# Counting edges in rings of six chunks, chunk totals in registers, five-row corrections widened to 96 rows, and the output bias added ahead

## The chip, the cores and the metric

The kernel runs on one core of a Trainium2 chip. The metric is the device time of one execution in microseconds (us), lower is better. The core has five engines that run side by side and meet at semaphores: TensorE (PE in the profile; its weight loads are PEld), VectorE (DVE), ScalarE (ACT), GpSimd (POOL) and SyncE (SP), which issues the DMAs.

## What is computed

A graph of N = 1250 nodes with 512 features and E = 21250 edges, sorted by destination. Four layers of conditioned layer norm, sparse four-head attention over the edges and a two-layer MLP come first; two graph convolutions follow. Cut to what matters here:

```python
x, src, dst, node_vec1 = _rec_inputs()         # (1250, 512), edges sorted by dst
h = jnp.maximum(_layernorm(x, axis=-1), 0.0)
x = x + _L0_gnn_ref(h, edge_index, ...)        # 4 blocks: attention over edges, MLP
h = jnp.maximum(_layernorm(x, axis=-1), 0.0)
x = x + _L1_gnn_ref(h, edge_index, W1, b1, W2, b2)

def _gcn_conv(x, src, dst, W, b, n):           # used twice, relu between
    h = x @ W
    deg = segment_sum(ones, dst)
    norm = rsqrt(deg)[src] * rsqrt(deg)[dst]
    return segment_sum(h[src] * norm, dst) + b
```

Edges are random pairs, so the kernel never gathers by edge. It first makes a dense 1250 x 1250 matrix that says how often each edge occurs, and both the attention and the graph convolutions are then dense products with it.

## The kernel before, in words

**Counting (span 12 to 175 us).** The nodes are ten tiles of 125, the edges 170 chunks of 125. A tile of destinations needs the chunks that hold them, found at run time: `tab` holds for each tile its first chunk and its number of turns, and for each tile from the third on the turns of earlier tiles of the same parity. For each chunk VectorE makes two one-hot matrices in bf16, `oh_dst` (125 edges x 125 nodes, L1105) and `oh_src` (125 edges x 1250 nodes, L1107), and TensorE multiplies them into a 125 x 1250 count in PSUM with three matmuls of 512, 512 and 226 columns (L1622). One turn of the loop (`one_hots` on VectorE, `count_tile` on TensorE) does `TRIO` = 3 chunks, so the chunks of a tile are rounded up to a multiple of three; surplus chunks count nothing. Even tiles use one ring of three slots, odd tiles another, so VectorE may be at most three chunks ahead within a tile, and it may begin the next tile with three chunks of the other ring. It waits on `oh_used0` or `oh_used1`, which TensorE raises after a chunk; TensorE waits on `onehot0` or `onehot1`.

Between two tiles TensorE closes the sum (L1627), turns the counts of the tile before into blocks (L1639), opens the next sum (L1610) and does one small matmul of the conditioning network (L1659, up to the eighth tile); ScalarE copies counts and blocks out, and SP writes the blocks to `counts_scratch` in DRAM. VectorE reads numbers of `tab` into registers (`value_load`, L1096 to L1098: three of them from the third tile on) and has small work of its own: the sines' arguments after the first tile, splits of the weights after the fifth to seventh, the first layer norm around the last two.

**The four layers (175 to 1640 us)** are not touched.

**The graph convolutions (1640 to 1885 us).** Float32 values go through TensorE as pairs of fp32r halves. The count matrix with self loops (`whole`) is one fp32r half; what is cut off is nonzero only in rows with large counts, at most `WIDE` = 5 rows, and that rest is one more small product. `gather_rows(j, p)` (L1903) is the first convolution's gather: for each of four feature groups j and three column pieces p, 20 matmuls of 125 rows. `add_rest(j, p)` (L1910) adds the rest with one matmul of 5 rows from `hs5[0]` and `rest5`. `last_rows(t)` (L1975) and `last_rest(t)` (L1980) do the same for the second convolution, once per node tile, with `hs5[1]`. Between them lies the product with the second weight (`product`, L1680), for which `rows_out` on ScalarE and `rows_low` on VectorE (L1381) make the two halves. GpSimd adds the self loops (L606) and fetches the five rows by index (L679). At the end VectorE scales each tile, adds the output bias `bvb` into `ztmp` (L1570), adds that to the running features `z` (L1573), and SP writes the tile out. TensorE goes on with tile t once `g_fin` says that bank t - 2 was read.

Each engine runs its instructions in the order written; nothing reorders them.

Of the kernel before, what the change touches and what calls it, by code (L numbers as in the profile page):

```python
# [14 lines left out]
ALU = mybir.AluOpType  # L15
# [9 lines left out]
N = 1250  # L25
# [5 lines left out]
C = 16  # L31
# [7 lines left out]
TRIO = 3  # L39
ECP = EC + TRIO  # L40
# [14 lines left out]
WIDE = 5  # L55
WIDE_AT = 4095.5


def build(nc, x, src, dst, node_vec1, f_w1, f_b1, f_w2, f_b2, s1_w, s1_b, b1_w, b1_b, wq, bq, wk, bk, wv, bv,
# [5 lines left out]
    with ExitStack() as ctx:  # L65
# [134 lines left out]
        rest5 = place("rest5", [WIDE, N], F32R, r_qg)  # L200
        hs5 = [place("hs5a", [WIDE, D], F32R, r_qc), place("hs5b", [WIDE, D], F32R, r_qg + 5024)]
# [12 lines left out]
        h1T = early("h1T", [C, N])  # L214
        oh_src = early("oh_src", [T, 2 * TRIO, N], BF16)
        oh_dst = early("oh_dst", [T, 2 * TRIO, T + 1], BF16)
        iota16 = early("iota16", [T, N], F16)
        iota_i = early("iota_i", [T, N], I32)
        zeros16 = early("zeros16", [T, D], BF16)
        edge_i = early("edge_i", [128, 4, T], I32)  # L220
        edge_f = early("edge_f", [128, 4, T])
        edgeT = early("edgeT", [T, 2, ECP])
        nb = early("nb", [2 * NFREQ, N])
# [45 lines left out]
        for name in ("x_ld edge_ld small_ld brow_ld ident consts edge_f edge_t edgeT brow_t cols emb_u emb_r emb_f emb emb_h "  # L269
# [7 lines left out]
                     "g_agT g_w2h g_w2 g_row g_tri g_wide g_gath g_h5 g_h5e g_b5 g_ft g_fin g_fz g_out z0 settled").split():  # L277
# [188 lines left out]
        def _(pool):  # L466
# [3 lines left out]
            for ring in range(2):  # L470
                pool.sem_inc(s[f"oh_used{ring}"], TRIO)
# [204 lines left out]
            for t in range(6, NT):  # L676
                self_loop(t)
            pool.wait_ge(s["g_wide"], 5)
# [349 lines left out]
        def _(dve):  # L1028
# [52 lines left out]
            tab_step(v.tensor_scalar(tab[:, 0:NT], R[2], float(ECP - TRIO), None, ALU.min))  # L1081
            tab_step(v.tensor_scalar(R[1], R[4], 1.0 / TRIO, 1.0 / TRIO, ALU.mult, ALU.add))
# [9 lines left out]

            def one_hots(t):

                ring = t % 2
                first = dve.value_load(tab[0:1, t:t + 1], min_val=0, max_val=ECP - TRIO)  # L1096
                trios = dve.value_load(tab[0:1, NT + t:NT + t + 1], min_val=1, max_val=EC // TRIO + 1)
                before = 0 if t < 2 else dve.value_load(tab[0:1, 2 * NT + t:2 * NT + t + 1], min_val=0, max_val=(EC // TRIO + 1) * NT)  # L1098
                with dve.Fori(0, trios) as i:
                    used = dve.snap((before + i) * TRIO)  # L1100
                    chunk0 = dve.snap((first + i * TRIO).with_bounds(min_val=0, max_val=ECP - TRIO))
                    for b in range(TRIO):
                        slot = ring * TRIO + b
# [432 lines left out]
            dve.wait_ge(s["g_b5"], 1)  # L1536
# [27 lines left out]
            for t in range(NT):  # L1564
                rows_low(NT + t, t % 2, t)
# [452 lines left out]
```

## Time and profile before

| | us |
|---|---|
| median of three runs | 1888.9 (1887.29 to 1889.1) |
| the profiled execution | 1887.38 |
| its span | 1885.5 |
| TensorE busy | 1823.2 (97%) |
| VectorE busy | 1382.1 (73%) |
| ScalarE busy | 826.0 (44%) |
| GpSimd busy | 450.9 (24%) |
| mean granted TensorE clock | 0.995 |

The profile is of one execution. TensorE is busy nearly throughout, so a microsecond is gained where TensorE waits, or where a group of its instructions takes longer than its columns need. The page cuts the span into 40 slices of 47 us; the first four show TensorE at 6, 9, 9 and 9 tenths, and the rest 9 or more but for the last. A busy time is not a peak, since matmuls overlap, so starts are a better measure of pace than durations.

### The profile page before, as it was taken

The page shows a single profiled execution, that of the slowest core. Times are in us where ns is not written, and L with a number is a line of the kernel's source. Part 1 is how long each engine was busy: PE and PEld are TensorE (multiplying, and loading weights), DVE is VectorE, ACT ScalarE, POOL GpSimd, SP SyncE. Part 2 cuts the span into 40 slices and gives each one's busy share as a digit, 9 for nine tenths or more (in the row PEclk, how much of TensorE's full clock was granted, in tenths as well). Part 3 has the DMA queues.
Part 4 walks back from the last instruction along what each step waited for, and adds up shares of the span by engine and source line. Part 5 has one row for each costly group of instructions (what it writes and reads, how often), then busy time and mean ns, then how long its engine had stood idle before and what let it go on. Part 6 is the DMA issues. An engine that isn't in the chain of part 4 may idle for free. (4 is left out here: it accounts for less than half of the span.)

```text
span 1885.5 us, 33968 instructions
## 1 busy us (share of the span) xinstructions
PE 1823.2 (97%) x11796; PEld 1570.6 (83%) x11796; DVE 1382.1 (73%) x2835; ACT 826.0 (44%) x1613; POOL 450.9 (24%) x544
## 2 busy tenths in 40 slices
PE   6998999999999999999999999999999999999998
PEld 3555988999889989998899899988998999877776
DVE  7887669888885498888854988888549888875323
ACT  1552455455442264554422555544225555446220
POOL 1000234111351341113513411125134111261000
PEclk9999999999999999999999999999999999999999
DMA  4112563111301121103011211030112110522001
GB/s 142 40 40 54 156 171 116 38 37 28 125 1 56 39 61 38 37 27 127 1 56 38 60 38 37 27 127 1 49 46 61 38 37 27 161 52 54 1 1 55
DMA packets 50752, 108.40 MB, mean 57 GB/s; under 512 B 18170, under 2 KB 18222, under 8 KB 50640
## 3 DMA queue, kind: packets, MB, share of 16 engines
q1 hardware_dynamic: 50608, 106.87, 19.4%
q8 instruction: 72, 1.18, 0.3%
q14 instruction: 40, 0.33, 0.1%
q0 software_dynamic: 32, 0.03, 0.0%
HBM read 83.62 MB, written 23.25 MB: 57 GB/s over the span
## 5 line engine op out<-in xcount | busy, mean ns | idle before, releaser
L871 ACT ACTIVATE PT<-ps 125x500 fp32r<-125x500 f32 (+1 forms) x480 | 214.2, 520 | 315.6 <-PE ps L1780 315.6
L1680 PE MATMUL ps<-PT,V 125*128 125x250 f32 x2400 | 313.3, 284 | 1.6 <-DVE PT L1279 1.6
L1680 PE MATMUL ps<-kT,qg 128*125 128x512 f32 (+1 forms) x1440 | 302.2, 355 | 6.1 <-DVE nmx L1263 5.2
L1680 PEld LDWEIGHTS ps<-kT,qg 128*125 128x125 f32 x1440 | 245.8, 187 | 55.4 <-issue 6.8
L1680 PEld LDWEIGHTS ps<-PT,V 125*128 125x128 f32 x2400 | 289.6, 190 | 2.9 <-DVE PT L1279 2.9
L1279 DVE TENSOR_TENSOR PT<-ps,PT 125x500 fp32r<-125x500 f32 (+1 forms) x480 | 253.2, 583 | 2.2 <-ACT PT L871 1.8
L1263 DVE CUSTOM_DVE_ANT_0 SB<-ps,bt 125x1250 f32<-125x1250 f32 x140 | 203.9, 1457 | 46.7 <-PE ps L1680 44.6
L1780 PE MATMUL ps<-ident,pbuf 125*125 125x125 f32 x1600 | 202.2, 274 | 10.3 <-DVE PT L1279 4.0
L1780 PEld LDWEIGHTS ps<-ident,pbuf 125*125 125x125 f32 x1600 | 187.3, 189 | 14.0 <-issue 9.3
L865 ACT ACTIVATE pbuf<-SB,nmx 125x1250 f32<-125x1250 f32 x140 | 188.1, 1344 | 11.0 <-DVE nmx L1263 9.7
L1272 DVE TENSOR_SCALAR pbuf<-pbuf,rden 125x1250 f32<-125x1250 f32 x160 | 149.9, 937 | 5.6
L542 POOL CAST qg<-qc 128x250 fp32r<-128x250 f32 x80 | 36.2, 453 | 443.4 <-PE ps L1680 408.3
L1680 PEld LDWEIGHTS ps<-yTb,wa 128*128 128x128 f32 x1152 | 136.7, 189 | 3.1 <-issue 1.3
L1680 PE MATMUL ps<-yTb,wa 128*128 128x250 f32 x1152 | 137.2, 279 | 1.1 <-DVE yTb L1228 1.1
L1622 PE MATMUL ps<-oh_src,oh_dst 125*125 125x512 bf16 x558 | 122.6, 374 | 9.4 <-DVE oh_src L1107 9.4
L1680 PE MATMUL ps<-wmS,hT 128*125 128x512 f32 x480 | 124.3, 403 | 3.4 <-POOL hT L613 3.1
L1622 PEld LDWEIGHTS ps<-oh_src,oh_dst 125*125 125x125 bf16 x558 | 67.3, 145 | 67.0 <-DVE oh_src L1107 45.1
L1680 PEld LDWEIGHTS ps<-yT,wmS 128*128 128x128 f32 x960 | 114.1, 189 | 4.2 <-issue 2.4
L1680 PE MATMUL ps<-yT,wmS 128*128 128x250 f32 x960 | 114.6, 278 | 2.0 <-DVE yT L1228 2.0
L1680 PEld LDWEIGHTS ps<-wmS,hT 128*125 128x125 f32 x480 | 84.6, 186 | 32.0 <-POOL hT L613 11.2
L1680 PE MATMUL ps<-WOS,outTg 128*125 128x512 f32 x320 | 102.3, 401 | 0.3
L1107 DVE TENSOR_SCALAR oh_src<-iota,edgeT 125x1250 bf16<-125x1250 f16 x186 | 101.9, 548 | 0.0
(243 smaller groups left out, 2811.0 us busy)
## 6 DMA issues: line engine op xcount, KB each, us to landing
bt<-edge_bias_scratch SPq DMA_DIRECT2D x40, 546.9 KB
q_scratch<-qc SPq DMA_DIRECT2D x16, 500.0 KB, 2.6
qc<-q_scratch SPq DMA_DIRECT2D x16, 500.0 KB, 4.7
counts_scratch<-cblk SPq DMA_DIRECT2D x10, 546.9 KB
c_rows<-counts_scratch SPq DMA_DIRECT2D x10, 546.9 KB
edge_bias_scratch<-b_rows SPq DMA_DIRECT2D x10, 546.9 KB
counts<-counts_scratch SPq DMA_DIRECT2D x10, 546.9 KB
wm<-in_L_gnn_wo_dram SPq DMA_DIRECT2D x4, 1024.0 KB, 8.6
```

The costliest lines, as they stand in the source:

```text
L542: g.tensor_copy(qg[:, 0, h, :], qc[:, h, :]).then_inc(s["qgh"], 1)
L865: sc.activation(P[:, u, :], SB[:, :] if own else P[:, u, :], ACT.Exp, bias=nmx[:, u:u + 1], scale=-1.0, accum_out=den[:, u:u + 1]).then_in ...
L871: sc.activation(PT[:, h % 2, 0, a:b, u * T:(u + 1) * T], ps_T[0:T, i, 0:(b - a) * T].rearrange("p (t n) -> p t n", n=T), ACT.Copy).then_in ...
L1107: v.tensor_scalar(oh_src[:, slot, :], iota16[:, :], edgeT[:, 0, bass.ds(chunk0 + b, 1)], None, ALU.is_equal).then_inc(s[f"onehot{ring}"], 1)
L1263: v.tensor_tensor_reduce(out=SB[:, :] if own else P[:, u, :], in0=banks, in1=bt[:, u, :], scale=-1.0, scalar=FLOOR, op0=ALU.add, op1=ALU.m ...
L1272: v.tensor_scalar(P[:, u, :], P[:, u, :], rden[:, u:u + 1], None, ALU.mult).then_inc(s["P"], 1)
L1279: v.tensor_tensor(o[:, 1], ps_T[0:T, i, 0:(b - a) * T].rearrange("p (t n) -> p t n", n=T), o[:, 0].bitcast(F32), ALU.subtract).then_inc(s[ ...
L1622: e = mm(psf[0:T, o + a:o + b], oh_dst[:, slot, 0:T], oh_src[:, slot, a:b], start=False, stop=False, skip_group_check=True)
L1680: e = mm(out_, lhs(a), rhs(b), start=start and i == 0, stop=stop and i == 2)
L1780: e = turn(ps_T[0:T, p, (m - a) * T:(m - a + 1) * T], P[:, u, m * T:(m + 1) * T], ident[0:T, 0:T])
```

## The change

Three things change.

1. `TRIO` becomes `SIX` = 6: a turn does six chunks, a ring has six slots, the chunks of a tile are rounded up to a multiple of six. VectorE no longer loads the earlier turns from `tab`; it adds the turn counts that it has in registers. TensorE still loads them. To make room `h1T`, `iota_i`, `edge_i` and `nb` move to memory that is used only later.
2. `rest5` and both `hs5` get `DEEP` = 96 rows, cleared to zero by GpSimd; VectorE writes five rows of them as before. The matmuls of L1910 and L1980 then have 96 rows. VectorE waits for the clearing (`g_z5`) ahead of its first copy into `wide_y`, which shares memory with `rest5`.
3. `z` gets the output bias tile by tile during the product with the second weight; at the end one instruction does `z = ps * dis + z` in place of two, and TensorE waits for `g_fz` in place of `g_fin`.

The diff, without the moved placements and the renamings:

```diff
-            tab_step(v.tensor_scalar(R[1], R[4], 1.0 / TRIO, 1.0 / TRIO, ALU.mult, ALU.add))
+            tab_step(v.tensor_scalar(R[1], R[4], 1.0 / SIX, 0.5 - 0.5 / SIX, ALU.mult, ALU.add))
...
+            turns, done_by = [], [0, 0]
+
             def one_hots(t):
 
                 ring = t % 2
-                first = dve.value_load(tab[0:1, t:t + 1], min_val=0, max_val=ECP - TRIO)
-                trios = dve.value_load(tab[0:1, NT + t:NT + t + 1], min_val=1, max_val=EC // TRIO + 1)
-                before = 0 if t < 2 else dve.value_load(tab[0:1, 2 * NT + t:2 * NT + t + 1], min_val=0, max_val=(EC // TRIO + 1) * NT)
-                with dve.Fori(0, trios) as i:
-                    used = dve.snap((before + i) * TRIO)
...
+                first = dve.value_load(tab[0:1, t:t + 1], min_val=0, max_val=ECP - SIX)
+                sixes = dve.value_load(tab[0:1, NT + t:NT + t + 1], min_val=1, max_val=EC // SIX + 1)
+                before = done_by[t] if t < 2 else dve.snap((done_by[t] + turns[t - 2]).with_bounds(min_val=0, max_val=(EC // SIX + 1) * NT))
+                turns.append(sixes)
+                done_by.append(before)
+                with dve.Fori(0, sixes) as i:
+                    used = dve.snap((before + i) * SIX)
...
             for t in range(6, NT):
                 self_loop(t)
+            g.memset(hs5[0][:, :].bitcast(F32), 0.0).then_inc(s["g_z5"], 1)
+            pool.wait_ge(s["g_hs_mm"], NT)
+            g.memset(rest5[:, :].bitcast(F32), 0.0).then_inc(s["g_z5"], 1)
+            g.memset(hs5[1][:, :].bitcast(F32), 0.0).then_inc(s["g_z5"], 1)
             pool.wait_ge(s["g_wide"], 5)
...
             dve.wait_ge(s["g_b5"], 1)
+            dve.wait_ge(s["g_z5"], 3)
             for p, (a, b) in enumerate(PIECES):
                 e = v.tensor_copy(wide_y[:, a * T:b * T], ps[0:WIDE, 3 + p, 0:(b - a) * T])
...
             for t in range(NT):
                 rows_low(NT + t, t % 2, t)
+                v.tensor_tensor(z[:, t, :], z[:, t, :], bvb[:, :], ALU.add).then_inc(s["g_fin"], 1)
             dve.wait_ge(s["g_h5"], 2)
-            v.tensor_copy(hs5[1][:, :], ps[0:WIDE, 2, :]).then_inc(s["g_h5e"], 1)
+            v.tensor_copy(hs5[1][0:WIDE, :], ps[0:WIDE, 2, :]).then_inc(s["g_h5e"], 1)
             for t in range(NT):
                 dve.wait_ge(s["g_ft"], t + 1)
-                v.scalar_tensor_tensor(out=ztmp[:, t % 2, :], in0=ps[0:T, t % 2, :], scalar=dis[:, t:t + 1], in1=bvb[:, :],
-                                       op0=ALU.mult, op1=ALU.add).then_inc(s["g_fin"], 1)
                 dve.wait_ge(s["g_fin"], t + 1)
-                v.tensor_tensor(z[:, t, :], z[:, t, :], ztmp[:, t % 2, :], ALU.add).then_inc(s["g_fz"], 1)
+                v.scalar_tensor_tensor(out=z[:, t, :], in0=ps[0:T, t % 2, :], scalar=dis[:, t:t + 1], in1=z[:, t, :],
+                                       op0=ALU.mult, op1=ALU.add).then_inc(s["g_fz"], 1)
...
-                    pe.wait_ge(s["g_fin"], t - 1)
+                    pe.wait_ge(s["g_fz"], t - 1)
```

How instructions stand on VectorE where the third tile's one-hots begin, before the change (TENSOR_LOAD and the ISA rows behind it are one `value_load`; the last rows are the first chunk):

```order
L1096 TENSOR_LOAD tab
L1096 ISA x2
L1097 TENSOR_LOAD tab
L1097 ISA x2
L1098 TENSOR_LOAD tab
L1098 ISA x2
L1099 UNCONDITIONAL_BRANCH
L1099 ISA
L1105 ISA
L1105 TENSOR_SCALAR oh_dst<-iota_148,edgeT 125x125
```

And with the change:

```order
L1103 TENSOR_LOAD tab
L1103 ISA x2
L1104 TENSOR_LOAD tab
L1104 ISA x2
L1108 UNCONDITIONAL_BRANCH
L1108 ISA
L1114 ISA
L1114 TENSOR_SCALAR oh_dst<-iota_148,edgeT 125x125
```

One of the three loads is gone. The rows of the loop behind it repeat a chunk six times in place of three.

GpSimd's last rows, before:

```order
L606 TENSOR_TENSOR counts_107<-counts_107,ident 125x125
L606 TENSOR_TENSOR counts_108<-counts_108,ident 125x125
L606 TENSOR_TENSOR counts_109<-counts_109,ident 125x125
L606 TENSOR_TENSOR counts_110<-counts_110,ident 125x125
L679 DMA wide_x<-counts_scratch,idx 5x1250
```

And with the change:

```order
L607 TENSOR_TENSOR counts_110<-counts_110,ident 125x125
L679 MEMSET hs5a 96x512
L681 MEMSET rest_134 96x1250
L682 MEMSET hs5b 96x512
L684 DMA wide_x<-counts_scratch,idx 5x1250
```

Three clears stand between the last self loop and the fetch of the five rows.

VectorE's end of the program, before (`agg_low`'s last row, the ten of `rows_low`, the five rows for the rest, then each tile's two steps):

```order
L1554 TENSOR_TENSOR aggL<-agg_123,aggH 128x226
L1381 SCALAR_TENSOR_TENSOR hsL<-ps,dis,hsH 125x512 x10
L1567 CAST hs5b<-ps 5x512
L1570 SCALAR_TENSOR_TENSOR ztmp<-ps,dis,bvb 125x512
L1573 TENSOR_TENSOR z<-z,ztmp 125x512
```

And with the change:

```order
L1390 SCALAR_TENSOR_TENSOR hsL<-ps,dis,hsH 125x512
L1576 TENSOR_TENSOR z<-z,bvb 125x512
L1578 CAST hs5b<-ps 5x512
L1582 SCALAR_TENSOR_TENSOR z<-ps,dis,z 125x512 x10
L66 UNCONDITIONAL_BRANCH
```

The ten additions to `z` moved from behind the last matmuls to between the ten steps of `rows_low`.

## Rows read from the trace of the kernel before

**Rows 1.** The page: busy time, share of the span and instructions.

```profile
PE 1823.2 (97%) x11796; PEld 1570.6 (83%) x11796; DVE 1382.1 (73%) x2835; ACT 826.0 (44%) x1613; POOL 450.9 (24%) x544
```

**Rows 2.** Counting: us, busy PE PEld DVE ACT POOL, clock, DMA share, GB/s.

```profile
12.00:175.00 163.00, 147.57 (x705) 82.45 (x706) 136.80 (x409) 59.61 (x111) 1.45 (x2) 0.96 0.23 63
```

**Rows 3.** Timeline of DVE, third tile: start, duration, engine, line, [idle before <- releaser].

```profile
47.05 0.26 DVE L1105 TENSOR_SCALAR oh_dst<-iota,edgeT 125x125 bf16<-125x125 f16 x1 [1.69 <-issue]
...
51.00 0.26 DVE L1105 TENSOR_SCALAR oh_dst<-iota,edgeT 125x125 bf16<-125x125 f16 x1 [2.00 <-PE ps L1622]
51.17 0.54 DVE L1107 TENSOR_SCALAR oh_src<-iota,edgeT 125x1250 bf16<-125x1250 f16 x1
...
59.81 0.54 DVE L1107 TENSOR_SCALAR oh_src<-iota,edgeT 125x1250 bf16<-125x1250 f16 x1
```

**Rows 4.** Timeline of PE and PEld, end of the third tile, start of the fourth.

```profile
60.40 0.41 PEld L1622 LDWEIGHTS ps<-oh_src,oh_dst 125*125 125x125 bf16 x3 [0.21 <-DVE oh_src L1107]
...
64.91 1.47 PEld L1622 LDWEIGHTS ps<-oh_src,oh_dst 125*125 125x125 bf16 x9 [0.85 <-DVE oh_src L1107]
64.91 11.16 PE L1622 MATMUL ps<-oh_src,oh_dst 125*125 125x512 bf16 x54
```

**Rows 5.** Waits by line, VectorE: us in total, times, longest.

```profile
DVE oh_dst L1105 <- PE ps L1622: 11.6, 19, 2.0
```

**Rows 6.** Timelines of DVE and PE where the clock was low.

```profile
19.93 0.26 DVE L1105 TENSOR_SCALAR oh_dst<-iota,edgeT 125x125 bf16<-125x125 f16 x1 [0.32 <-PE ps L1622]
20.98 0.26 DVE L1105 TENSOR_SCALAR oh_dst<-iota,edgeT 125x125 bf16<-125x125 f16 x1 [0.34 <-PE ps L1622]
...
127.64 13.74 PE L1622 MATMUL ps<-oh_src,oh_dst 125*125 125x512 bf16 x54 [2.07 <-DVE oh_src L1107]
...
146.67 14.37 PE L1622 MATMUL ps<-oh_src,oh_dst 125*125 125x512 bf16 x63 [2.44 <-DVE oh_src L1107]
```

**Rows 7.** Sequencer instructions of lines 1098 (DVE) and 1616 (PE): duration ns min/median/max.

```profile
L1098 DVEq TENSOR_LOAD <-tab x8: 298/298/311, 46.0 to 162.2; - x8
L1098 DVEq FUSED_REGOPS  x8: 183/183/183, 46.4 to 162.6; - x8
L1098 DVEq SEQ_ASSERT  x8: 23/23/23, 46.6 to 163.2; - x8
L1616 PEldq COMPARE_BRANCH  x62: 76/207/241, 17.7 to 175.0; - x62
```

**Rows 8.** The chain that ended last, first convolution's gather: start, us, what.

```profile
1739.99 4.63 PE ps L1903 x20
...
1776.69 0.42 PE ps L1910
1777.11 4.83 PE ps L1903 x20
1781.94 0.42 PE ps L1910
```

**Rows 9.** Timeline of PE: matmuls of 96 rows among matmuls of 128 rows.

```profile
207.99 1.11 PE L1691 MATMUL ps<-lnS,condc 96*125 96x512 f32 x4
208.94 0.97 PE L1680 MATMUL ps<-yT,wa 128*128 128x250 f32 x7
```

**Rows 10.** GpSimd's last self loop and a 96-row clear; VectorE's first copy into wide_y.

```profile
1714.18 0.46 POOL L606 TENSOR_TENSOR counts<-counts,ident 125x125 f32<-125x125 f32 x1 [1.38 <-DMA counts<-counts_scratch]
...
L505 POOL MEMSET condS<- 96x1250 f32 x1 | 1.1, 1141 | 0.1
...
1756.28 1.57 DVE L1538 COPY wide_y<-ps 5x500 f32<-5x500 f32 x3 [4.42 <-PE ps L1936]
```

**Rows 11.** Timeline of DVE: rows_low's last step, and the end of the program.

```profile
1827.13 0.75 DVE L1381 SCALAR_TENSOR_TENSOR hsL<-ps,dis,hsH 125x512 fp32r<-125x512 f32 x1 [2.04 <-ACT hsH L925]
...
1881.35 0.75 DVE L1570 SCALAR_TENSOR_TENSOR ztmp<-ps,dis,bvb 125x512 f32<-125x512 f32 x1 [3.78 <-PE ps L1980]
1882.13 0.69 DVE L1573 TENSOR_TENSOR z<-z,ztmp 125x512 f32<-125x512 f32 x1
```

More of the change, by code:

```diff
@@ L199, in build @@
         wide_y = place("wide_y", [WIDE, N], F32, r_qg)
-        rest5 = place("rest5", [WIDE, N], F32R, r_qg)
-        hs5 = [place("hs5a", [WIDE, D], F32R, r_qc), place("hs5b", [WIDE, D], F32R, r_qg + 5024)]
+        rest5 = place("rest5", [DEEP, N], F32R, r_qg)
+        hs5 = [place("hs5a", [DEEP, D], F32R, r_qc), place("hs5b", [DEEP, D], F32R, r_qg + 5024)]
         in_pb = packer(r_pb + 4 * 4 * D, r_pb + 4 * 2 * N)
@@ L276, in build @@
                      "g_cnt g_c6 g_c7 g_c8 g_c9 g_x zx g_xd g_nb g_eye g_H g_dg g_diag g_bc g_disb g_hs_mm g_hh g_hs g_ag g_agd g_agr g_agh "
-                     "g_agT g_w2h g_w2 g_row g_tri g_wide g_gath g_h5 g_h5e g_b5 g_ft g_fin g_fz g_out z0 settled").split():
+                     "g_agT g_w2h g_w2 g_row g_tri g_wide g_gath g_h5 g_h5e g_b5 g_ft g_z5 g_fin g_fz g_out z0 settled").split():
             s[name] = sem(name)
@@ L470, in _ @@
             for ring in range(2):
[L471 removed]
+                pool.sem_inc(s[f"oh_used{ring}"], SIX)
             g.memset(ident[:, :], 0.0).then_inc(s["ident"], 1)
@@ L1091, in _ @@
             dve.wait_ge(s["prefix"], 3)
+            turns, done_by = [], [0, 0]
             def one_hots(t):
                 ring = t % 2
[L1096 to L1103 removed]
+                first = dve.value_load(tab[0:1, t:t + 1], min_val=0, max_val=ECP - SIX)
[5 more added lines that the diff above has]
+                    used = dve.snap((before + i) * SIX)
+                    chunk0 = dve.snap((first + i * SIX).with_bounds(min_val=0, max_val=ECP - SIX))
+                    for b in range(SIX):
+                        slot = ring * SIX + b
                         dve.wait_ge(s[f"oh_used{ring}"], used + (b + 1))
@@ L1611, in open_counts, with count_tile @@
                        skip_group_check=True)
-            def count_tile(t, trios, before):
+            def count_tile(t, sixes, before):
                 ring, o = t % 2, ACC[t % 2]
-                with pe.Fori(0, trios) as i:
-                    done = pe.snap((before + i) * TRIO)
-                    for q in range(TRIO):
-                        slot = ring * TRIO + q
+                with pe.Fori(0, sixes) as i:
+                    done = pe.snap((before + i) * SIX)
+                    for q in range(SIX):
+                        slot = ring * SIX + q
                         pe.wait_ge(s[f"onehot{ring}"], done + (q + 1))
@@ L1663, in _ @@
                 open_counts(t)
-                ahead = trios_ahead(t)
+                ahead = sixes_ahead(t)
                 if t >= 2:
```

29 lines of the change are left out of this document (15 added, 14 removed).

## The prediction, written before the changed kernel ran

> **What bounds the kernel now.** I read the page first: TensorE is busy for 97% of the span, VectorE for 73% [rows 1], so over the whole program TensorE is the bound. The change touches the counting and the last 150 us, so I went on by stretch. In the counting [rows 2] TensorE is busy 147.6 of 163 us and VectorE 136.8, so neither is plainly the bound, and the timeline has to tell. It shows VectorE going from chunk to chunk in 0.617 us ((59.81 - 51.17) / 14) [rows 3], with TensorE behind it, idle 0.21 us before each chunk's first weight load [rows 4]: within a tile VectorE sets the pace. Between tiles it is otherwise. VectorE makes three chunks of the next tile, then waits 2.00 us for a slot [rows 3], since TensorE begins the tile 4.51 us after its last chunk began (64.91 - 60.40) [rows 4]. So a full tile takes neither engine's own time but the sum of pieces of both: the third tile starts on VectorE at 47.05 and the fourth 1.7 us after 60.35 (59.81 + 0.54), 15.0 us apart, of which 18 chunks are 11.1 [rows 3]. The waits for slots are 11.6 us in 19 times [rows 5]. From 1740 us on the chain is TensorE alone [rows 8], with one step of VectorE at its end [rows 11].
>
> **Deeper rings.** How many chunks there are: 186 before, eight tiles of 18 and two of 21 (x54 and x63 are three matmuls per chunk) [rows 4, 6]. A tile of 18 needed 16 to 18, one of 21 needed 19 to 21; in sixes these become 18 and 24. That adds 6 chunks of 0.617: +3.7 us.
>
> Waits removed: the 11.6 us are idle time alone. A normal chunk starts 0.09 us before the one ahead ends (0.617 against 0.17 + 0.54) [rows 3], which a wait loses too, and some waits are too short to be listed; start against start, over all 186 pairs, I get 14.2 us. Of these 7.3 stand at the starts of tiles 3 to 7 (2.1 at the third, 51.00 - 47.05 - 3 x 0.617 [rows 3], then 2.0, 1.4, 1.6 and 0.2), and 6.9 in stretches in which TensorE ran at 1.2 GHz. There a chunk takes it 1.05 us (20.98 - 19.93) [rows 6] against 0.617 on VectorE, and three slots are soon full. Each such stretch lasted four to seven chunks, so TensorE falls back by at most 7 x 0.43 = 3.0 us, which three more slots (1.9 us) and the slack of the first three nearly cover: I count all 6.9 us as removed.
>
> At the starts of tiles not all goes. At full clock TensorE needs 0.50 us per chunk by its weight loads (9 in 1.47) [rows 4], and 0.57 if I count the columns at the float32 gather's pace (4.63 / 20 per 512) [rows 8]; I take 0.53, between the two. A tile then costs TensorE at least 4.51 + 17 x 0.53 = 13.5 us, and VectorE 18 x 0.617 + about 1.2 for its register loads = 12.3. So in tiles 3 to 6 TensorE becomes the bound and VectorE waits again at its seventh chunk: with six chunks made (3.7 us) and a slot free about 1.0 us after TensorE has begun the tile, I get 0.85, 1.2, 0.6 and 0.2 us, in all 2.8. From the seventh tile on VectorE's own insertions and the extra chunks keep it behind, and it does not wait. Removed, then: 14.2 - 2.8 = 11.4 us.
>
> What could eat into this is TensorE's own loop: a backward branch is 0.21 us on its sequencer [rows 7], which is hidden now because TensorE waits for VectorE anyway. With some bookkeeping it is up to 0.3 us for each of three turns in four tiles, 3.5 us in all; I take nothing, since the branches are issued while queued matmuls still run, and keep 3.5 for the range. On the other side 0.50 us per chunk would give at most 17 x 0.03 x 4 = 2 us more.
>
> **Turn counts in registers.** One value_load less is 0.298 + 0.183 + 0.023 us [rows 7] and the gaps between; three of them and the branch make the 1.69 us idle [rows 3], so one is 0.5 to 0.6: I take 0.58. It counts at eight tile starts, but twice it lies under a split of 2.29 us that is still running, so 6 x 0.58 = 3.5 us less. The addition in its place is one register operation. If the queue in front of VectorE hid the load, it would be worth nothing; the 1.69 us of idle says that it does not.
>
> Counting together: -11.4 - 3.5 + 3.7 = -11.2 us. What follows (GpSimd's wait for the last blocks in DRAM, the first layer's loads) hangs on the last tile and moves with it. The moved placements only take memory whose users come later in program order; I cost them at 0, and their semaphores are the old ones.
>
> **96 rows.** A rest matmul of 5 rows begins at 1776.69 and the next at 1781.94, 5.25 us for 20 gather matmuls and one rest; at the pace of the first run (4.63 for 20, 0.2315 each) 21 would take 4.86 [rows 8]. So each place where 5-row matmuls stand among 125-row ones costs 0.39 us, for one or for three in a row, by going in and coming out. There are 17 such places: 8 in the first gather (two groups of three, six alone) and 9 in the last (a pair, eight alone), and the last has no way out. 96 rows do not show this: four of 96 rows among 128-row matmuls take 0.95 us, 0.2375 each [rows 9]. So 16 x 0.385 + 0.19 = 6.3 us less, all of it on TensorE's chain. The bounds are 0 (if the 96-row row does not carry over) and 6.6.
>
> The Trainium skill speaks against this step. By its page TensorE: Matmul & The Clock Gate, section "Why this matters for your kernels", a lone matmul of 32 rows takes the time of one of 128, so the row count alone should buy nothing. By that rule this term would be 0 and the whole 6.3 us smaller in gain; the starts in rows 8 disagree for 5 rows between 125-row neighbours, and I go by them.
>
> GpSimd's clears: its last self loop ends at 1714.6, a 96 x 1250 clear takes 1.14 us, one of 512 columns about 0.5 [rows 10]. The first is free at once; the other two wait for the last `nodes` product, which ends at 1739.99 where the gather begins [rows 8], so they are over by 1741.7. VectorE needs them at 1756.28 [rows 10], 14.6 us later. Behind the clears only the fetch of five rows is queued on GpSimd, and it waits for the same engine's index until 1752. Cost 0; were the cover gone, TensorE's second feature group would wait too, since it needs the banks that VectorE copies out.
>
> **Bias ahead.** Ten additions of 0.69 us [rows 11] go between the steps of rows_low, which take 0.75 us and stand 2.8 us apart with 2.04 idle [rows 11]. They fit: 1.44 of 2.8. The last ends before 1829, and VectorE's next work (five rows of hs5) came at 1833.4. Cost 0; without that cover, 6.9 us. At the end one step of 0.69 us and its gap go: 1882.13 - 1881.35 = -0.8 us. That TensorE waits for g_fz in place of g_fin is the same instruction's end.
>
> **The sum.** -11.2 - 6.3 - 0.8 = -18.3 us on an execution of 1887.4 us (span 1885.5): 1869.1. The median of the runs shown is 1.5 us above the profiled execution, so I forecast 1870.6 us.
>
> **Rivals.** (a) *TensorE's turns show.* With more chunks ready TensorE is the bound and its branches cost the 3.5 us above: 1874.1. For it: TensorE never ran more than a few chunks unhindered here, so its loop has not been seen at full pace. Against it: half as many branches.
> (b) *96 rows gain nothing*, because the cost is in changing the operands' source and not in five rows: 1876.9. Against it: rows 9.
> (c) *Slower: the low clock stays.* In the counting TensorE fell to 1.2 GHz after it had stood idle for 2.07 and for 2.44 us [rows 6]. If the new rhythm kept it low, a tile would take 18 x (1.05 - 0.617) = 7.8 us more. It decides from the third such tile on (18.3 / 7.8 = 2.3); with five it is 1909 us. Against it: the waits of TensorE become shorter, and in tiles 3 to 6 there are none.
> (d) *The rings bring nothing*: something else holds a tile at 15 us, for instance ScalarE's copies between tiles; then only the load, the 96 rows and the bias gain, and 3.7 are lost: 1870.6 + 11.4 = 1882.0. Against it: VectorE's waits name TensorE's matmuls of the same ring.
>
> **Chances and range.** The forecast 0.74, (a) 0.11, (b) 0.07, (c) 0.03, (d) 0.03, and 0.02 for no difference. The forecast's own range is 1867.5 to 1873.5: 2 us for the pace per chunk and 1 for the load. To hold 8 of 10 I go up to (b) and down by one stretch of low clock that no longer comes: 1866 to 1877. A change of this kernel can be told from none by 0.2%, 3.8 us. Faster 0.95 (all but (c) and the last), same 0.02, slower 0.03.
>
> **What would show it.** In the changed profile: 192 pairs of one-hots, VectorE's waits on the counting matmuls down from 11.6 us to some 3 and only at a tile's seventh chunk; 1.1 us idle by issue at tile starts; the counting over 11 us earlier; from one rest matmul to the next 4.86 us; the last steps on VectorE one of 0.75 us. The prediction is wrong if the seventh chunk waits longer than 1.5 us, if the stretch from the first gather matmul to the end is not 7 us shorter, or if TensorE runs the counting at half clock.

## The result, and the profile after

The changed kernel takes 1871.03 us (median of 4 runs, 1869.86 to 1872.21) against 1889.0 us for the kernel before on the same chip (4 runs, 1887.29 to 1889.28): ratio 0.9908, 95% interval 0.9895 to 0.992. That is 18 us less, and the forecast was 1870.6. The profiled execution took 1871.84 us with a span of 1870.1 (before: 1887.38 and 1885.5), so between the two profiles the difference is only 15.5 us. Step by step, as markers in the two traces (us from the span's start):

| | before | after | shift |
|---|---|---|---|
| last pair of one-hots begins on VectorE | 174.14 | 162.19 | -11.95 |
| TensorE's conditioning chunk behind the count blocks' landing (L1701) begins | 189.46 | 178.95 | -10.51 |
| first convolution's gather begins | 1739.83 | 1729.60 | -10.23 |
| W2's product begins | 1798.25 | 1786.68 | -11.57 |
| last gather begins | 1826.21 | 1814.56 | -11.65 |
| last step of VectorE ends | 1882.83 | 1867.39 | -15.44 |

First the page of the changed kernel, its busy times and counts, beside [rows 1]:

```profile
PE 1810.0 (97%) x11814; PEld 1575.5 (84%) x11814; DVE 1382.6 (74%) x2847; ACT 826.5 (44%) x1613; POOL 453.8 (24%) x547
```

TensorE runs 18 matmuls more (six extra chunks) and still is 13 us less busy, VectorE has 12 operations more. (In the page of the kernel before, the fourth of the 40 slices shows TensorE at 8 tenths, not 9; with the change the first four are 6, 9, 8 and 8.) The counting by stretch, as in [rows 2], the same columns:

```profile
12.00:175.00 163.00, 148.40 (x791) 94.65 (x792) 144.67 (x436) 65.76 (x125) 1.82 (x2) 0.98 0.28 71
```

In the same 163 us 86 more matmuls fit in, since the first layer has begun by then; VectorE's busy time rises from 136.8 to 144.7. The waits of VectorE, by line, over the counting (us in total, times, longest), which answer [rows 5]:

```profile
DVE oh_dst L1114 <- issue: 6.8, 7, 1.9
DVE oh_dst L1114 <- PE ps L1632: 4.7, 3, 1.9
```

Nineteen waits for slots are now three, and they are where the prediction put them, at the seventh chunk of tiles 3, 4 and 5. But look at how long they are, and at what is missing ahead of the tiles. VectorE's timeline with the change, the waits of tiles 3 to 5, to be set beside [rows 3] (start, duration, line, in brackets the idle time before):

```profile
48.05 0.26 DVE L1114 TENSOR_SCALAR oh_dst<-iota,edgeT 125x125 bf16<-125x125 f16 x1 [1.94 <-PE ps L1632]
...
55.82 0.26 DVE L1114 TENSOR_SCALAR oh_dst<-iota,edgeT 125x125 bf16<-125x125 f16 x1 [0.26 <-issue]
...
61.30 0.26 DVE L1114 TENSOR_SCALAR oh_dst<-iota,edgeT 125x125 bf16<-125x125 f16 x1 [1.69 <-PE ps L1632]
...
69.22 0.26 DVE L1114 TENSOR_SCALAR oh_dst<-iota,edgeT 125x125 bf16<-125x125 f16 x1 [0.35 <-issue]
...
74.07 0.26 DVE L1114 TENSOR_SCALAR oh_dst<-iota,edgeT 125x125 bf16<-125x125 f16 x1 [1.05 <-PE ps L1632]
```

The third tile has no idle time at its start at all (it begins at 42.33, six chunks of 0.617 before the wait), the fourth and fifth 0.26 and 0.35 us, where there were 1.7 us before. TensorE's weight loads of the third tile and its matmuls, answering [rows 4]:

```profile
47.05 9.47 PEld L1632 LDWEIGHTS ps<-oh_src,oh_dst 125*125 125x125 bf16 x54 [0.85 <-issue]
```

```profile
47.05 9.81 PE L1632 MATMUL ps<-oh_src,oh_dst 125*125 125x512 bf16 x54
...
60.29 5.99 PE L1632 MATMUL ps<-oh_src,oh_dst 125*125 125x512 bf16 x32
```

Eighteen chunks in one unbroken group of 54: 9.47 / 18 = 0.53 us each, through three turns of the loop. From the third tile to the fourth TensorE takes 60.29 - 47.05 = 13.2 us instead of 15.

The first gather, its chain in order of time (start, us, what), beside [rows 8]:

```profile
1736.46 6.30 PE ps L1913 x20
...
1762.64 4.65 PE ps L1913 x20
1767.29 0.24 PE ps L1920
1767.52 4.64 PE ps L1913 x20
1772.16 0.24 PE ps L1920
```

From one rest matmul to the next it is 1772.16 - 1767.29 = 4.87 us, against 5.25 before; the rest matmul itself counts 0.24 us instead of 0.42. The first row shown is a trap: 20 gather matmuls in 6.30 us, because the granted clock stood at its lower level (1.2 GHz) for 3.4 us from 1737.7 on. GpSimd's clears, by start, duration and line, answering [rows 10], read 1705.60 0.52 (L679), 1729.82 1.14 (L681) and 1730.90 0.53 (L682): the last two began as the gather began, and VectorE did not wait for them. And VectorE at the end, answering [rows 11]:

```profile
1815.48 0.75 DVE L1390 SCALAR_TENSOR_TENSOR hsL<-ps,dis,hsH 125x512 fp32r<-125x512 f32 x1 [1.44 <-ACT hsH L930]
1816.15 0.68 DVE L1576 TENSOR_TENSOR z<-z,bvb 125x512 f32<-125x512 f32 x1
...
1861.79 0.75 DVE L1582 SCALAR_TENSOR_TENSOR z<-ps,dis,z 125x512 f32<-125x512 f32 x1 [4.13 <-PE ps L1990]
1866.64 0.75 DVE L1582 SCALAR_TENSOR_TENSOR z<-ps,dis,z 125x512 f32<-125x512 f32 x1 [4.10 <-PE ps L1990]
```

The bias additions sit in what was idle time, and the steps of the last gather are 4.85 us apart.

### The profile page after: what moved, and what is told of

Read it like the earlier page. It is cut to its first block and busy times, and to the rows that moved or that the text cites. A ratio compares the mean times of both kernels' runs of the same rounds, so it can differ in the third digit from the quotient of the medians.

```text
span 1870.1 us, 33910 instructions
## 1 busy us (share of the span) xinstructions
PE 1810.0 (97%) x11814; PEld 1575.5 (84%) x11814; DVE 1382.6 (74%) x2847; ACT 826.5 (44%) x1613; POOL 453.8 (24%) x547
## 5 line engine op out<-in xcount | busy, mean ns | idle before, releaser
L1690 PEld LDWEIGHTS ps<-yTb,wa 128*128 128x128 f32 x1152 | 136.8, 189 | 3.1 <-issue 1.3
L1632 PE MATMUL ps<-oh_src,oh_dst 125*125 125x512 bf16 (+1 forms) x576 | 115.4, 358 | 6.9 <-DVE oh_src L1116 6.9
L1632 PEld LDWEIGHTS ps<-oh_src,oh_dst 125*125 125x125 bf16 x576 | 71.1, 142 | 53.3 <-DVE oh_src L1116 26.0
```

Source lines behind the costliest of these rows:

```text
L1632: e = mm(psf[0:T, o + a:o + b], oh_dst[:, slot, 0:T], oh_src[:, slot, a:b], start=False, stop=False, skip_group_check=True)
L1690: e = mm(out_, lhs(a), rhs(b), start=start and i == 0, stop=stop and i == 2)
```

## The experiments

Twelve kernels ran, in three groups of four, each group on a chip of its own; the kernel before ran with each group (medians 1886.73, 1886.48 and 1888.13 us). A figure in brackets is the 95% interval of a ratio to it.

### Each part alone

**The rings alone** (with the turn counts in registers and the moved placements; the rest as before; lines of the edit against the changed kernel):

```diff
-        rest5 = place("rest5", [DEEP, N], F32R, r_qg)
+        rest5 = place("rest5", [WIDE, N], F32R, r_qg)
...
-                v.tensor_tensor(z[:, t, :], z[:, t, :], bvb[:, :], ALU.add).then_inc(s["g_fin"], 1)
```

> The kernel before with the rings of six and the turn counts in registers alone; 5-row rests and the two last steps as before. My theory: the trace of the changed kernel has its last pair of one-hots 12.0 us earlier than before, of which 1.4 us were lost again behind it, when TensorE waited 1.79 in place of 0.43 us for GpSimd and the last blocks in DRAM. If that loss is the ring's doing (blocks arrive closer together), this kernel gains 10.5 us: 1878.5. If it is chance of one execution, it gains up to 12: 1877. By rival (d) of the prediction it gains nothing or loses: 1885 or more. The wait for the last blocks in its profile tells the first two apart: 1.8 us again, or 0.4.

Measured: 1876.42 us, ratio 0.9947 [0.9934, 0.996], so 10.3 us less. Its last pair begins at 162.16, as in the full change, with the same two waiting rows (6.8 and 4.7 us). The question about the last blocks is answered too: here they land 6.55 us after their copy, and TensorE does not wait at that chunk, so the 1.79 us of the first profile are not the ring's doing. The gather has the row of 6.30 us.

**96 rows alone** (kernel before, with the diff's hunks on `rest5`, `hs5` and the three clears):

```diff
-            v.tensor_copy(hs5[0][:, :], ps[0:WIDE, 6, :]).then_inc(s["g_h5e"], 1)
+            v.tensor_copy(hs5[0][0:WIDE, :], ps[0:WIDE, 6, :]).then_inc(s["g_h5e"], 1)
```

> The kernel before with the 96-row rests alone. My theory: 17 places lose 0.385 us each, 6.1 to 6.3 us less, 1882.8; from one rest matmul to the next 4.87 us. By rival (b), the row count alone buys nothing: 1889. A second question is the stretch of low clock that the changed kernel had in the gather, 1737.7 to 1741.1 us, which cost it 1.6 us: if the 96 rows bring it, it is here too, at the same place in the program; if it hangs on what happened before, it is not, and the gain is the full 6.2.

Measured: 1880.92 us, 0.9967 [0.9954, 0.998], 5.8 us less. Its chain in the first gather:

```profile
1771.65 4.65 PE ps L1909 x20
1776.30 0.24 PE ps L1916
1776.53 4.64 PE ps L1909 x20
1781.17 0.24 PE ps L1916
```

The 4.87 us from rest to rest come with this edit and nothing else. The second question of the expectation, the low clock in the gather, is answered by a row further ahead in the same chain:

```profile
1745.47 6.30 PE ps L1909 x20
```

The granted clock is at its lower level for 3.4 us from 1746.8 on, 8.2 us behind the gather's start and at the same place in the program as in the changed kernel. So in this profile too the first gather has 1.6 us of the gain taken back.

**The bias alone:**

```diff
+                v.tensor_tensor(z[:, t, :], z[:, t, :], bvb[:, :], ALU.add).then_inc(s["g_fin"], 1)
...
-                v.tensor_tensor(z[:, t, :], z[:, t, :], ztmp[:, t % 2, :], ALU.add).then_inc(s["g_fz"], 1)
+                v.scalar_tensor_tensor(out=z[:, t, :], in0=ps[0:T, t % 2, :], scalar=dis[:, t:t + 1], in1=z[:, t, :],
+                                       op0=ALU.mult, op1=ALU.add).then_inc(s["g_fz"], 1)
```

> The kernel before with the output bias added ahead alone. My theory: 0.7 to 0.8 us less, 1888.2, below what can be measured in the median, but plain in the profile as one step of 0.75 us at the end in place of 0.75 and 0.69. A rival: the ten additions get in the way of the steps of rows_low or of the last matmuls, and it is slower by more than 1 us.

Measured: 1885.39 us, 0.9995 [0.9987, 1.0004]: 1.3 us less, with an interval that holds both no change and the 0.8 us expected. The three parts add up to 10.3 + 5.8 + 1.3 = 17.4 us, the whole change gives 18.0: no interaction between them shows above the noise.

**The full change with the register load put back:**

```diff
-                before = done_by[t] if t < 2 else dve.snap((done_by[t] + turns[t - 2]).with_bounds(min_val=0, max_val=(EC // SIX + 1) * NT))
+                before = 0 if t < 2 else dve.value_load(tab[0:1, 2 * NT + t:2 * NT + t + 1], min_val=0, max_val=(EC // SIX + 1) * NT)
```

> The changed kernel with the third register load put back (rings of six and all else stay). The prediction's term: 6 exposed loads of 0.58 us, 3.5 us slower than the changed kernel, 1874.5. The rival from the changed trace: in tiles 3 to 6 TensorE is the bound, so there the load is hidden by the six chunks that are ready or by the wait at the seventh; only the last three tiles are set by VectorE, and it costs 3 x 0.6 = 1.8 us, 1872.9. The wait at the seventh chunk tells: if it shrinks by the load's 0.6 us in tiles 3 to 5, the rival is right.

Measured: 1870.37 us, 0.9917 [0.9904, 0.9929]: 16.4 us less than before where the full change has 18.0. The medians differ by less than the intervals; the traces are sharper. The last pair begins at 164.14 instead of 162.19, 1.95 us later. The start of tile 4 and its seventh chunk in this kernel, then the starts of tiles 8 to 10:

```profile
56.44 0.26 DVE L1114 TENSOR_SCALAR oh_dst<-iota,edgeT 125x125 bf16<-125x125 f16 x1 [0.86 <-issue]
61.33 0.26 DVE L1114 TENSOR_SCALAR oh_dst<-iota,edgeT 125x125 bf16<-125x125 f16 x1 [1.08 <-PE ps L1632]
...
118.77 0.26 DVE L1114 TENSOR_SCALAR oh_dst<-iota,edgeT 125x125 bf16<-125x125 f16 x1 [2.15 <-issue]
135.29 0.26 DVE L1114 TENSOR_SCALAR oh_dst<-iota,edgeT 125x125 bf16<-125x125 f16 x1 [2.12 <-issue]
153.65 0.26 DVE L1114 TENSOR_SCALAR oh_dst<-iota,edgeT 125x125 bf16<-125x125 f16 x1 [1.72 <-issue]
```

The starts of tiles 8 to 10 in the changed kernel:

```profile
118.22 0.26 DVE L1114 TENSOR_SCALAR oh_dst<-iota,edgeT 125x125 bf16<-125x125 f16 x1 [1.64 <-issue]
...
134.23 0.26 DVE L1114 TENSOR_SCALAR oh_dst<-iota,edgeT 125x125 bf16<-125x125 f16 x1 [1.61 <-issue]
...
151.70 0.26 DVE L1114 TENSOR_SCALAR oh_dst<-iota,edgeT 125x125 bf16<-125x125 f16 x1 [0.84 <-issue]
```

Tile 4 is the lesson. With the third load 0.86 + 1.08 = 1.94 us are idle, without it 0.26 + 1.69 = 1.95 (rows above): the load was paid out of the wait behind it, and the seventh chunk begins at 61.33 or 61.30. Only in the last three tiles, where VectorE is the late engine, does it show: 2.15, 2.12 and 1.72 us against 1.64, 1.61 and 0.84, in all 1.9 us. This is what the expectation's rival said, and not the prediction's term.

### The depth of the ring and the rounding

Both edit one number of the full change:

```diff
-SIX = 6
+SIX = 3
```

> The changed kernel with three chunks per turn and three slots per ring again, turn counts still in registers, 96-row rests and early bias kept: it takes the depth away and the rounding with it. My theory after the first four runs: the depth is nearly all of the counting's gain. With three slots the starts of tiles 3 to 7 are held by the slot wait whatever the loads cost, so the missing load shows in tiles 8 to 10 only. Expected: last one-hot pair at 170 to 172.5 us (the kernel before: 172 to 174.1 in three profiles; the changed kernel 162.1), 186 pairs, waits for slots 11 to 12 us again, the whole 8.5 us slower than the changed kernel, 1878.5. By the prediction's term (six loads exposed, 3.5 us) it would be only 6.5 slower.

Measured for three: 1877.4 us, 0.9952 [0.9938, 0.9965]. VectorE's waits, and its operations:

```profile
L1116 DVE TENSOR_SCALAR oh_src<-iota,edgeT 125x1250 bf16<-125x1250 f16 x186 | 101.5, 546 | 0.0
L1114 DVE TENSOR_SCALAR oh_dst<-iota,edgeT 125x125 bf16<-125x125 f16 x186 | 47.2, 254 | 24.4 <-PE ps L1632 14.2 <-issue 9.5
```

Slots are waited for 22 times again, 14.2 us, and the last pair begins at 174.60, later than the 170 to 172.5 expected. At the third tile the two waits are now

```profile
47.56 0.26 DVE L1114 TENSOR_SCALAR oh_dst<-iota,edgeT 125x125 bf16<-125x125 f16 x1 [1.08 <-issue]
...
52.12 0.26 DVE L1114 TENSOR_SCALAR oh_dst<-iota,edgeT 125x125 bf16<-125x125 f16 x1 [2.61 <-PE ps L1632]
```

against 1.69 and 2.00 before [rows 3]: the load is gone from the first and comes back in the second. The same trade stands at tiles 4 and 5. At tiles 8 to 10 the idle time falls from 2.15, 2.11 and 1.70 to 1.66, 1.62 and 0.83 us, 1.85 us that no slot wait takes back. That the last pair is late all the same goes in part with the clock, which was at its lower level five times for 3.4 us in this counting and four times in that of the kernel before; the rest is not separated. By medians the edit leaves 9.1 us of gain, of which 96 rows and bias are 7.1, so the load is at most 2; the depth and its rounding are then worth the other 8.9 of the 18.0 us (expected 8.5).

```diff
-SIX = 6
+SIX = 5
```

> The changed kernel with five chunks per turn and five slots. Tiles of 16 to 18 chunks become 20, those of 19 to 21 become 20 or 25: 200 to 210 pairs. It prices the rounding. If a surplus chunk costs VectorE's 0.617 us throughout, 8 more pairs (200) put the last pair 4.9 us later than in the changed kernel, at 167.1, and 18 more (210) at 173.2; if surplus chunks are free where TensorE is the bound they would cost less, but there TensorE's own 0.53 per chunk holds, 4.3 and 9.5 us. A loss well above 0.62 per extra pair would mean that a fifth slot is not enough and depth still counts.

Measured for five (2 runs): 1877.37 us, 0.9952 [0.9934, 0.9971]. The same two rows:

```profile
L1116 DVE TENSOR_SCALAR oh_src<-iota,edgeT 125x1250 bf16<-125x1250 f16 x200 | 108.6, 543 | 0.0
L1114 DVE TENSOR_SCALAR oh_dst<-iota,edgeT 125x125 bf16<-125x125 f16 x200 | 51.6, 258 | 13.9 <-PE ps L1632 7.1 <-issue 6.5
```

Five slots leave more waiting for slots than six (7.1 against 4.7 us; idle by issue is 6.5 against 6.8), and a tile of 16 to 18 chunks rounded up to fives takes 20, so 200 pairs are made: 8 x 0.617 = 4.9 us more. The last pair begins at 170.08, 7.9 us later than with six, or 0.99 us per extra pair. That is well above 0.62, so by the expectation's own test depth still counts: of the 3.0 us beyond the rounding 2.4 are slot waits, now at the sixth chunk (2.55, 2.37 and 1.30 us in tiles 3 to 5). Six is good here because it is deeper and because 18 is a multiple of it.

### How many rows a lone matmul must have

```diff
-DEEP = 96
+DEEP = 32
```

> The changed kernel with the rests cleared to 32 rows in place of 96. If what costs is how few rows the rest has, 32 rows should be nearer to 96 than to 5. If what costs is a way of using the array that goes with up to 32 rows, the rest of 32 rows costs the same as that of 5: 0.39 us at each of 17 places, 5.25 us from one rest to the next, 6.1 us slower than the changed kernel.

Measured (2 runs): 1876.72 us, 0.9949 [0.9931, 0.9967]. Its chain in the first gather:

```profile
1760.12 4.83 PE ps L1913 x20
1764.95 0.42 PE ps L1920
1765.37 4.83 PE ps L1913 x20
1770.20 0.42 PE ps L1920
```

> The changed kernel with the rests cleared to 64 rows. By the theory that a smaller part of the array is used and the change between parts costs, 64 rows (half) cost as much as 32, 5.25 us from rest to rest; by the theory that the cost falls with the rows, it is between 4.87 and 5.25.

With `DEEP = 64` (2 runs): 1874.8 us, 0.9939 [0.9921, 0.9957], and

```profile
1760.53 4.84 PE ps L1913 x20
1765.37 0.42 PE ps L1920
1765.79 4.83 PE ps L1913 x20
1770.62 0.42 PE ps L1920
```

From rest to rest it is 5.25 us with 32 rows and with 64, the same as with 5. From the first gather matmul to VectorE's last step it is 143.9 us with 32 rows, in an execution with the row of 6.30 us, and 142.4 with 64, in one without it; with 96 rows it is 137.8 with that row (changed kernel) and 136.2 without (the kernel with the load put back): 6.1 us between them in both pairs, as expected. The medians, of two runs each, are 5.7 and 3.8 us above that of the changed kernel. So what costs 0.39 us is no matter of how few rows there are: 64 rows, 59 of them zero, gain nothing, 96 gain all. The Trainium skill, page TensorEngine Tiling (Array Packing), section "Tiling Modes", says that changing the tiling mode drains TensorE. The three depths agree with that, if 96 rows run in the mode of 125 and 64 do not; the page gives no duration, and here it is 0.39 us for going in and coming out.

### The changed kernel again, and two ways on

> The changed kernel once more, as the measure for the three kernels beside it and to see what an execution of it can vary. Theory: its counting ends at the same place each time (last one-hot pair at 162.1 us), while the landing of the last count blocks (9.0 us in the first profile, 6.6 to 7.5 in other kernels) and the number of 3.4 us stretches at the low clock differ from one execution to the next; so the median is again 1869 to 1873 us and the profiled execution may lie 1 to 3 us to either side of it. Rival: the 9.0 us landing and the low-clock stretch at the head of the gather belong to this kernel; then this profile shows both again, at 8.5 us or more and within 10 us of the gather's start.

Measured: 1870.25 us (1869.95 to 1871.03), 0.9908 [0.9892, 0.9925]. The last pair begins at 162.15. From the last block's copy to GpSimd's operation behind its landing it is 7.39 us here, 9.02 in the first profile; TensorE's wait at that place is 0.17 instead of 1.79. So the theory holds for the landing. For the low clock the rival holds: the stretch is there again, from 1736.1 on, 8.1 us behind the gather's start as in the first profile, and so is the one 58 us ahead of it (1678.1 here, 1679.7 there). Two executions of two are no proof that it belongs to the kernel, but it is no single accident.

**Loads ahead of their tiles.** If a load is free where VectorE's sequencer is ahead of its engine, the three exposed starts can be cured by their place in the code:

```diff
+            def load_turns(t):
...
+                if t not in ready:
+                    load_turns(t)
+                first, sixes, before = ready[t]
...
                 if t == 6:
+                    load_turns(7)
                     node_rstd()
                 if t == 7:
                     cond_low()
+                    load_turns(8)
+                    load_turns(9)
```

> VectorE's register loads of the last three tiles are issued earlier: those of tile 8 ahead of the square-root steps of the node statistics, those of tiles 9 and 10 (counted from one) right behind the conditioning row's low part. Theory: a load costs nothing where VectorE's sequencer is ahead of its engine, and 1.64, 1.61 and 0.84 us are idle at the starts of these three tiles only because the sequencer has caught up there. With the loads under long operations the idle time falls to a loop start of some 0.3 us each: last pair at 159 to 160 us, median 2.5 to 3.5 us under the changed kernel beside it. Rival: these tiles are held by TensorE all the same (it is at most a ring behind), so what VectorE gains is waited away at the seventh chunk: last pair at 161.5 or later and under 1 us gained.

Measured: 1866.3 us (1866.15 to 1866.53), 0.9887 [0.987, 0.9903]. The starts of tiles 8 and 9 in this kernel:

```profile
116.89 0.26 DVE L1123 TENSOR_SCALAR oh_dst<-iota,edgeT 125x125 bf16<-125x125 f16 x1 [0.38 <-issue]
131.89 0.26 DVE L1123 TENSOR_SCALAR oh_dst<-iota,edgeT 125x125 bf16<-125x125 f16 x1 [0.35 <-issue]
```

0.38 and 0.35 us where there were 1.64 and 1.61, and no gap at tile 10. The waits for slots stay at 4.7 us and the last pair begins at 158.91, 3.24 us earlier: the theory, and the rival falls. Of the 3.95 us between the medians these 3.24 are explained; the rest is within what the low clock moves (the stretch at the gather's head is absent here, which is 1.6 us in the profile).

**GpSimd's wait for the count blocks one chunk later:**

```diff
+                    if l == 0 and n == 0:
+                        for i in range(2):
+                            pool.wait_ge(s[f"cnt_out{i}"], NT * 16)
                     v_split(l, n)
...
-            for i in range(2):
-                pool.wait_ge(s[f"cnt_out{i}"], NT * 16)
```

> GpSimd's wait for the landing of the count blocks stands one conditioning chunk later, so that its first operation of layer 0 no longer stands behind it. Theory: in the changed kernel's profile TensorE waits 1.79 us for that operation because the landing took 9.0 us; where the landing takes about 6.7 us the wait is 0.4 to 0.9 us. Moved, the wait is gone whatever the landing takes: median 0.4 to 1.8 us under the changed kernel beside it, 0.9 likeliest. Rival: the next thing TensorE needs is late by the same amount (the low part of the first normalised block, written by VectorE), and nothing is gained: within 0.4 us.

Measured: 1868.54 us (1868.14 to 1869.11), 0.99 [0.9883, 0.9916], 1.7 us under the changed kernel beside it. TensorE at this place, in this kernel and then in the changed kernel's first profile:

```profile
171.28 5.87 PE L1691 MATMUL ps<-yTb,wa 128*128 128x250 f32 x48 [1.12 <-DVE yTb L1238]
176.99 1.08 PE L1702 MATMUL ps<-lnS,condc 96*125 96x512 f32 x4
```

```profile
171.29 5.87 PE L1690 MATMUL ps<-yTb,wa 128*128 128x250 f32 x48 [1.12 <-DVE yTb L1237]
178.95 1.19 PE L1701 MATMUL ps<-lnS,condc 96*125 96x512 f32 x4 [1.79 <-POOL condc L527]
```

The wait is gone. Against the profile of the changed kernel beside it (177.31) that is only 0.3 us, so most of the 1.7 us are not this wait: 1.6 us of the profiles' difference are again the low clock at the gather's head, absent here. Worth of the wait: 0.3 to 1.9 us, by how long the landing takes.

> The loads ahead and GpSimd's wait later, in one kernel. Theory: the two places lie one behind the other in time and add up: 3 + 0.9 = 3.9 us under the changed kernel beside it, so 1866 to 1868.5 us, the fastest of all here. Rival: with the counting over earlier the weights' and conditioning's preparation on GpSimd and ScalarE is late instead, and of the 3.9 us less than 2 are left.

Measured: 1866.75 us (1865.45 to 1869.59), 0.9894 [0.9878, 0.9911]. That is 3.5 us under the changed kernel beside it and inside the expected 1866 to 1868.5, but not the fastest of all: it cannot be told from the loads alone. In the profiles the two do add (last pair 158.85; conditioning chunk at 173.58 against 174.41; end at 1860.97 against 1861.79), so 0.8 us are there and drown in these four runs. In this execution the gather ran at the higher level of the clock (2.4 GHz):

```profile
1731.60 4.74 PE ps L1926 x20
```

That row answers the 6.30 above. The two kernels with the loads ahead are the fastest of all here, faster than both the kernel before and the changed one.

## Why the prediction came true, and which terms were off

*What bounds.* Right. A tile took pieces of both engines, and with six slots tiles 3 to 5 are TensorE's: 12.8 to 13.2 us from start to start, forecast 13.5.

*Counting: forecast -11.2, measured -12.0.* Two errors nearly cancel.

- The rings were forecast at -11.4 + 3.7 = -7.7 us. Measured without the load's part (the kernel with the load put back, last pair 164.14 against 174.14) they give -10.0. The step that failed is "in all 2.8" for the waits that stay, and more than that what stands at the tiles' starts: I left all idle time by issue as it was. With three loads per tile and six slots VectorE waits 3.5 us for slots (0.7 more than forecast), but idle by issue falls from 13.0 to 9.8 us (3.2 less).
- The load was forecast at -3.5 and is worth -2.0. The sentence "the 1.69 us of idle says that it does not" (hide) was the mistake: it read the shallow ring's state as a property of the load. The profile's rows on VectorE's sequencer, changed kernel, tile 3 (duration min/median/max in ns, first and last start in us), with the first load and the second:

```profile
L1103 DVEq TENSOR_LOAD <-tab x1: 300/300/300, 40.0 to 40.0; - x1
...
L1104 DVEq TENSOR_LOAD <-tab x1: 311/311/311, 40.6 to 40.6; - x1
```

The tile's first one-hot begins at 42.33, 2.3 us later. In the kernel before, the first load of that tile was

```profile
L1096 DVEq TENSOR_LOAD <-tab x1: 303/303/303, 44.8 to 44.8; - x1
```

issued when the engine was at its last pair of one-hots (44.82 to 45.36), so that the tile began only at 47.05 [rows 3]. The loads lie ahead only where no wait just ahead has held the sequencer back; with three slots it is held nearly at the engine, with six it runs on for chunks. A wait for a slot is not the only kind: at tile 8 of the changed kernel none stands near, but the first load is issued at 116.42, with the last of six short steps that each need the one ahead (the last at 116.40, 0.17 us), and 1.64 us are idle. The gain moved: idle by issue 9.8 to 6.8 us with the load gone (-3.0), of which 1.2 come back as waits at the seventh chunk (3.5 to 4.7).

- The -12.0 and the -10.0 hang on one execution of the kernel before. In two other profiles with the old counting, 96 rows alone and the bias alone, the last pair begins at 172.86 and 171.99 and the waits for slots are 10.6 and 10.1 us instead of 11.6. Against those the counting gains 10.7 and 9.8 us, and the rings without the load's part 8.7 and 7.9. The rings alone, with the load's part, gained 10.3 in the medians. So that the rings beat their forecast by 2.3 us is shown for the profiled execution and no further.

By its own tests the prediction was wrong in two points. The seventh chunk waits 1.94 and 1.69 us, longer than the 1.5 I had set, for that reason: VectorE arrives early, and TensorE's start of the tile has not moved with it. And the stretch from the first gather matmul to the end is 5.2 us shorter, not 7 (below).

*Low clock in the counting.* 6.9 us were to go. The granted clock over the stretch is 0.98 against 0.96, and no wait for a slot stands outside tiles 3 to 5. Right, and not because the low clock was absent: the first profile of the changed kernel has two stretches of 3.4 us in the counting (four before), that of the load put back three, and neither has a slot wait outside tiles 3 to 5. In six profiles with the changed counting and one or two such stretches the last pair begins within 0.1 us of the same place. (The row at 19.93 us from which the prediction took the pace of 1.05 us lies ahead of the first clock record of its trace, 21.2 us; TensorE's chunks that begin at 36.04 and 37.08, 1.04 us apart, lie where the record shows the lower level.)

*Rival (a), TensorE's turns*: refuted, 0.53 us per chunk through the loop's turns. *(b), 96 rows gain nothing*: refuted by 96 rows alone. The rule of the Trainium skill that I weighed (page TensorE: Matmul & The Clock Gate, section "Why this matters for your kernels": one matmul of 32 rows takes the time of one of 128) is not contradicted by the time of a lone matmul, which no run here took by itself; but among 125-row neighbours it does not carry. *(c)*: refuted by the clock. *(d), the rings bring nothing*: refuted by the rings alone.

*96 rows: forecast -6.3.* Measured -2.9 in the first gather, -0.1 on the way out, -3.1 in the last: -6.1 in the profiles (5.8 by medians). Right.

*Bias: forecast -0.8*, measured -0.7 in the profiles. Right, and below what the medians can tell.

*What was to be 7 us shorter.* From the first gather matmul to the end it was 143.0 us and is 137.8, so 5.2. The missing 1.6 us are the gather's low-clock stretch, a cost I had not listed; in the last kernel above, without it, the same stretch takes 1860.97 - 1724.73 = 136.2, so 6.8 less.

*Sum.* The profiles give -12.0 + 1.4 (longer landing) + 0.3 (layers) - 2.9 + 1.6 (gather, low clock) - 0.1 - 3.1 - 0.7 = -15.5; the medians -18.0. The terms that were forecast come to -18.8 in the profiles (forecast -18.3), and 3.3 us stand against them that the prediction had not listed. That the medians differ by 18.0 all the same is in part luck: the profiled execution of the kernel before was 1.6 us under its median and that of the changed kernel 0.8 us over. The terms were right to within a few us; that 1870.6 met 1871.03 to half a us is chance.

*Left open.* Why the low clock comes at the gather's head in some kernels (the changed one both times, the rings alone, 96 rows alone, 32 rows; each time 8.0 to 8.2 us behind the gather's start) and not in the other nine profiles. TensorE works without a break there. Neither the rings nor the 96 rows are needed for it, since each had it without the other, and both together do not ensure it, since the kernel with the load put back has both and does not show it. Where it is absent there is always a stretch 35 to 36 us ahead of the gather, within 1 us of the end of a 2.1 us wait of TensorE, and where it is present that one is absent. Only one kernel was profiled twice, so whether a kernel fixes this or an execution is not shown.

## What to carry to other kernels

A ring between two engines should hold about what one engine makes while the other pauses between tiles or falls back at a low clock (here 4.5 us, some 7 chunks), and its depth should divide the length of the tiles, or the rounding eats the gain (five slots for tiles of 18 cost 4.9 us in surplus chunks). Idle time at a loop's start is no fixed price of its register loads: ask whether a wait just ahead has held the engine's sequencer back, and place the loads under a long operation. A few stray rows among full-height matmuls cost by the change in height, so fill them with zeros up to a height that the trace shows to be free, and try that height, since 64 was not enough here.

## What the runs showed of the hardware

- Matmuls of 5, 32 and 64 rows among ones of 125 cost the same 0.39 us per visit (5.25 us from rest to rest), 96 rows nothing (4.87).
- A register load from SBUF is about 0.3 us for the load, 0.2 for the register operation and 0.02 for the range assertion, and each costs nothing when the sequencer is 2.3 us ahead of its engine. The Trainium skill, page DMA: Bandwidth & Descriptors, section "Latency and other measured facts", has about 600 ns as the floor of a `tensor_load`. The traces agree only if the register operation and the assertion are counted with it (0.6 us from start to start, 40.0 to 40.6); the load's own row is half of that.
- The landing of the same last blocks took 6.6 to 9.0 us from execution to execution, and TensorE waited for it at one place for anything from nothing to 1.8 us.
- In five of fourteen profiles TensorE fell to the lower level of its clock for 3.4 us in the middle of unbroken matmul work in the gather, which made 20 matmuls take 6.30 instead of 4.74 us.
